# GpSimd issues the moves of the row maxima, SyncE keeps the moves of rows, and one key projection stands two steps sooner

## The reference

```
x = x + 0.5 * ffn(layernorm(x))            # 256 -> 2 x 768 -> 256, silu(gate) * up, int weights
x = x + attention(layernorm(x))            # 16 heads of 16, ALiBi bias -slope * |l - s|
x = x + 0.5 * ffn(layernorm(x))

attention(x): q, k, v = x Wq', x Wk', x Wv'
              scores = q k' / 4 + bias;  out = softmax(scores) v;  out Wo' + bo
```

## Time and profile before

| | |
|---|---|
| time, median of 3 runs | 805.88 us (804.81 to 812.14) |
| profiled execution | 807.18 us, of which the span from first to last instruction is 805.3 us |
| mean granted TensorE clock | 0.993 |
| busy: PE / DVE / ACT / POOL | 758.7 / 618.4 / 521.4 / 450.8 us |
| DMA queue of SP | 41.92 MB, 28.0% of 16 engines' span |

### The profile page before, as it was taken

How to read it: one execution, slowest core, us unless ns; L and a number is a source line. 1 busy time by engine, 2 the same in 40 slices (tenths; PEclk the granted TensorE clock), 3 DMA queues, 4 the chain that set the end, 5 groups by cost and what they waited for, 6 DMA issues and landing times.

```text
span 805.3 us, 13303 instructions
## 1 busy us (share of the span) xinstructions
PE 758.7 (94%) x4576; PEld 467.0 (58%) x4576; DVE 618.4 (77%) x1267; ACT 521.4 (65%) x1001; POOL 450.8 (56%) x550
## 2 busy tenths in 40 slices
PE   2999999999989999999999999999999997999998
PEld 1778887775443354444444454454443376988887
DVE  6698877967889968879878888879989076467763
ACT  5344444335868978878879879789788754344443
POOL 0433355425656767767766776767766555344433
PEclk9999999998999999999999999999999999999999
DMA  9440015401441650730721622522520000000001
GB/s 355 160 63 3 2 30 76 56 2 25 73 67 23 92 69 3 110 51 7 114 42 30 93 41 41 81 42 50 72 41 3 2 2 28 28 29 28 29 28 54
DMA packets 21637, 43.20 MB, mean 54 GB/s; under 512 B 3864, under 2 KB 5928, under 8 KB 21352
## 3 DMA queue, kind: packets, MB, share of 16 engines
q1 hardware_dynamic: 21544, 41.92, 28.0%
HBM read 12.02 MB, written 4.62 MB: 21 GB/s over the span
## 4 chain that ended last, share of the span: by engine, by line
PE 79%; ACT 7%; DVE 7%; issue 4%; DMA 1%; POOL 1%; DVEq 0%; ACTq 0%
PE ps L1003 73%; ACT probs L685 4%; PE ps L1066 2%; DVE row_max L881 2%; PE ps L1015 2%; DVE hid L811 1%; ACT stage L634 1%; PE ps L1071 1%; DMA q_aug<-parts 1%; DVE w_max L892 1%; ACT heads_t L669 1%; ACT xnt L652 1%; PE ps L1061 1%; DVE newton L732 1%; DMA x_sb<-x_in 0%
## 5 line engine op out<-in xcount | busy, mean ns | idle before, releaser
L881 DVE TENSOR_REDUCE row_max<-ps 128x1 f32<-128x512 f32 x512 | 326.6, 683 | 65.1 <-PE ps L1003 64.0
L685 ACT ACTIVATE probs<-ps 128x512 f32<-128x512 f32 x512 | 287.2, 607 | 49.3 <-PE ps L1003 47.6
L553 POOL TENSOR_TENSOR probs<-probs,diag 128x256 f32<-128x256 f32 x256 | 186.7, 731 | 131.7 <-ACT probs L685 130.9
L471 POOL TENSOR_TENSOR hid_r<-hid,hid_r 128x512 fp32r<-128x512 f32 x96 | 124.3, 1299 | 181.2 <-ACT hid_r L580 180.9
L1003 PE MATMUL ps<-k_aug,q_aug 60*128 60x512 f32 x512 | 191.3, 455 | 8.7 <-issue 3.8
L1003 PE MATMUL ps<-xnt,wgu_r 128*128 128x512 f32 x768 | 190.3, 402 | 7.9 <-issue 4.1
L1003 PE MATMUL ps<-q_aug,k_aug 62*128 62x512 f32 x512 | 191.6, 450 | 2.8 <-ACT probs L685 1.9
L1003 PEld LDWEIGHTS ps<-xnt,wgu_r 128*128 128x128 f32 x768 | 143.0, 190 | 46.3 <-issue 7.6
L1003 PEld LDWEIGHTS ps<-q_aug,k_aug 62*128 62x128 f32 x512 | 78.2, 186 | 120.6 <-ACT probs L685 97.6
L586 ACT ACTIVATE gated<-ps 128x512 f32<-128x512 f32 x96 | 57.4, 598 | 126.3 <-PE ps L1003 126.3
L1003 PE MATMUL ps<-probs,v_aug 128*32 128x512 f32 x1024 | 137.0, 608 | 0.1
(11 more groups left out here) (72 smaller groups left out, 672.3 us busy)
## 6 DMA issues: line engine op xcount, KB each, us to landing
q_aug<-parts SPq DMA_DIRECT2D x96, 128.0 KB, 4.6
k_aug<-parts SPq DMA_DIRECT2D x96, 128.0 KB, 4.6
x_sb<-x_in SPq DMA_DIRECT2D x8, 512.0 KB, 12.7
x_out<-x_sb SPq DMA_DIRECT2D x7, 512.0 KB, 2.6
diag<-diag_table SPq DMA_DIRECT2D x1, 2048.0 KB, 19.0
wgu_i<-w_gate_up SPq DMA_DIRECT2D x2, 768.0 KB, 6.0
w_att<-w_att SPq DMA_DIRECT2D x1, 1024.0 KB, 11.1
q_aug<-max_parts SPq DMA_DIRECT2D x64, 8.0 KB
```

Of the source, the lines that this page charges most:

```text
L471: nc.gpsimd.tensor_tensor(hid_r[:, 1, f, :], hid[:, f % 2, :], hid_r[:, 0, f, :].bitcast(F32), ALU.subtract).then_inc(s["hid_lo"], 1)
L553: nc.gpsimd.tensor_tensor(tile, tile, diag[:, kt % 2, n * QH + 2 * pair:n * QH + 2 * pair + 2, :], ALU.mult).then_inc(fixed, 1)
L685: nc.scalar.activation(probs[:, kt % 2, 2 * pair + i, :], score_bank(2 * g + i), ACT.Exp, scale=SLOPE_UNITS[pair]).then_inc(exp_done, 1)
L881: nc.vector.reduce_max(row_max[:, quad % 2, i, pair, t:t + 1], max_bank(b * MAX_TILES + tile), mybir.AxisListType.X).then_inc(s1_used, 1)
```

## The change

`move_max` leaves SyncE's program and is put, unchanged in what it moves, into GpSimd's, right behind `split_max`. SyncE's loop then holds only the row moves, in the order `qk0`, `qk1`, `qk2`, `qk3`. In the table of fills `qk1_next` and `turn0_prev` exchange their places: the key projection stands at (1, 1), the turn at (1, 3).

```diff
 FILLS = {
-    (1, 1): "turn0_prev", (1, 3): "qk1_next", (1, 4): "max2", (1, 5): "heads0", (1, 7): "qk2_next",
+    (1, 1): "qk1_next", (1, 3): "turn0_prev", (1, 4): "max2", (1, 5): "heads0", (1, 7): "qk2_next",
...
 (SyncE)
-            move_max(-1, "max0_next")
             sp.wait_ge(ffn[0]["y_used"], 2 * B)
             lay_k_rows(1)
             for b in range(B):
-                move_max(b, "max1")
                 if not last(b):
                     wait(sp, st_done, b * (2 * NQ * STEPS))
-                    move_rows(b, "qk0_next")
-                move_max(b, "max2")
-                if not last(b):
-                    move_rows(b, "qk1_next")
-                    move_rows(b, "qk2_next")
-                move_max(b, "max3")
-                if not last(b):
-                    move_rows(b, "qk3_next")
-                    move_max(b, "max0_next")
+                    for part in range(4):
+                        move_rows(b, f"qk{part}_next")
...
 (GpSimd)
+            def move_max(b, name):
+                seq, kind, part = fill_parts(b, name)
+                pool.wait_ge(max_split, seq * NQ + part + 1)
+                for o in range(2):
+                    at = ROW_MAX + o
+                    nc.gpsimd.dma_start(q_aug[seq % 2][at:at + GROUP + 1:GROUP, 2 * part:2 * part + 2, :].bitcast(F32).rearrange("i j (t p) -> i (j t) p", p=P),
+                                 max_parts[:, o, :].bitcast(F32)).then_inc(max_moved, 16)
...
             split_max(-1, "max0_next")
+            move_max(-1, "max0_next")
...
                         if s == 3 and FILLS[n, 4] in fills_of(b):
                             split_max(b, FILLS[n, 4])
+                            move_max(b, FILLS[n, 4])
```

More of the change, by code:

```diff
@@ L409, in move_rows @@
                                      ).then_inc(rows_moved[is_k], 16)
[L411 to L418, removed]
             lay_q_rows(0)
```

## The result

The changed kernel takes 848.35 us (median of 4 runs, 846.56 to 849.05) beside 807.18 us of the kernel before (4 runs, 804.81 to 812.14). The ratio is 1.0477 [1.0434, 1.0519]: 4.8% slower, where 0.4% had been forecast and a range of 798.9 to 828 us. The profiled execution took 846.56 us, with a span of 844.7 us.

The account below looks back on a forecast made before the run. TensorE was taken to set the pace; 10.7 us lost to late fixes against 7.1 us gained from its holes made 3.6 us slower, put on the 805.88 us median: 809.5 us, range 798.9 to 828 us.

Parts of the forecast that it names:

- the maxima's own deadline: At quad 2's first scores: maxima issued by GpSimd land at 333.0 us, 0.5 us in time.
- the maxima land late: Rival: maxima meet key rows, 0.2 us, hidden; or land 1 us later in every quad, 816 us; chance 0.05.
- late fixes: Fixes of steps 4 and 5 behind GpSimd's issues delay TensorE's weighing at the next quad's step 0; 10.7 us lost.
- Gain: TensorE's idle holes before tile 64 (quad 2, step 3) in blocks 0 to 5 vanish: 7.09 us won.
- The exchange costs nothing: Swapping the fills at (1, 1) and (1, 3) leaves TensorE the same matmuls within four steps; no cost found.
- The price of an issue on GpSimd: GpSimd's time for one DMA issue of the maxima, after `split_max`: estimated 1.04 us, between 0.549 and 1.288 us.
- T: GpSimd's delay per quad after `split_max`: two issues plus the wait for its own subtraction, 2.15 us.
- covers: Time between the end of step 5's fix and its weighing on TensorE, 1.05 to 2.27 us by quad.
- The cheap issue: Rival: a GpSimd issue costs SyncE's 0.549 us, T is 1.18 us, 7.0 us gain stay, 798.9 us; chance 0.22.
- The dear issue: Rival: a GpSimd issue costs 1.288 us, GpSimd bounds the turn of quads, 18.0 us slower, 823.9 us; chance 0.28.
- VectorE holding GpSimd: Rival: VectorE's layer-norm tiles at quad 1, step 4 delay GpSimd's issues, 4.9 us more, 814.4 us; chance 0.03.
- The key rows did come sooner: Denies the rival that GpSimd's work at (1, 1) or the queue holds the key rows, 813.6 us; chance 0.04.

Follow-up runs that it names:

- e2_sync_keys_first: Against the kernel before: the two fills exchanged, SyncE issues everything, all key DMAs ahead of `max2`; 836.0 us, ratio 1.0333.
- e4_split1: Against the kernel before: fills exchanged, SyncE issues everything, one key DMA ahead of `max2` and five behind; 800.68 us, ratio 0.9873; repeated 800.71 us, 0.9898.
- e1_no_swap: Against the changed kernel: the two fills put back, GpSimd still issues the maxima; 830.3 us, ratio 1.0255 to the kernel before.
- e9_pool_split1: Against the changed kernel: SyncE sends one key DMA, waits for the split of `max2`, sends five; 818.98 us, ratio 1.0131 to the kernel before.
- e5_half_keys: Against the changed kernel: only half the rows of each `qk1` DMA moved from block 1 on; 834.2 us, ratio 1.0355 to the kernel before.

## Why the prediction was wrong

**The step that failed** is the maxima's own deadline, and with it the rival "the maxima land late". The prediction let the moves land at most 1.1 us after their issue, taken from the kernel before, and priced their meeting with the key rows at one 128 KB DMA, 0.64 us, hidden. They met the rest of the query rows and all six key DMAs. In block 2 the issues end at 339.28 us and the maxima land 6.3 us later, not 1.1 us. The 0.64 us were the pace of issue; at the 126 to 129 GB/s of the windows 128 KB take 1.0 us. So the twelve row DMAs, issued in 7.6 us, need some 12.3 us to move (an estimate from these two numbers), and what is issued behind them finds what is left. TensorE's wait for the maxima, 25.0 us in all, is the first term; the mechanism had been given a chance of 0.05. The order on one queue alone makes it too (`e2_sync_keys_first`), and one key DMA instead of six takes it away (`e4_split1`).

The row that speaks against the forecast was in it: the earlier trace rows was read as saying that the query rows are over by 330 us and so cannot slow the keys. But the keys were to start at 327.4 us, and from 326 to 328 us the engines of the kernel before were still full of query rows, as its window there shows:

```profile
326.00:328.00 2.00, 2.00 (x14) 0.47 (x13) 1.08 (x3) 1.86 (x4) 1.03 (x2) 1.00 1.06 124
```

And the earlier trace rows says as much that the maxima had empty engines, and that the `max2` ahead of `qk1` on SP was not only a delay for the keys but what kept those engines empty. Moving the keys 3.6 us ahead put them there.

**The second term had no place in the sum**: a stalled TensorE. After waits of 3.2 to 4.2 us the clock is at its lower level for 3 to 10 us, and TensorE's busy time rises by 17.9 us. The prediction counted waits only.

**That it forecast "slower" at all** is luck: its 3.6 us came from late fixes against the holes. As measured, 3.6 us of late fixes, 2.7 us for `heads0` and 7.1 us gained make 0.8 us faster. The slowdown is the wait and the clock, which the sum did not hold.

**Gain**: right. None of the holes before tile 64 is left in blocks 0 to 5, and the key rows are issued right behind the query rows. The changed kernel alone does not prove it, since TensorE comes to tile 64 later there, behind its wait for the maxima; `e4_split1`, without that wait, shows that the gain is to be had.

**The exchange costs nothing**: not quite. `heads0` now comes before ScalarE has taken `max_row`, 0.44 us in six of the blocks, 2.7 us in all by the waits; alone, the exchange measures 1.0016 [0.9986, 1.0046].

**The price of an issue on GpSimd**: mis-sized upwards, 1.04 us forecast, 0.584 us measured in the median; T is 0.30 + 1.16 = 1.46 us, not 2.15 us. The 1.0 us that the prediction also tried is not a hold of GpSimd: with free engines the first packet moves 1.2 us after the issue begins (`e1_no_swap`), and as late after an issue on SyncE in the kernel before. By the prediction's covers a T of 1.46 us loses 0.05 us before the weighing of quad 0 of the next block, nothing in quad 1 and 0.41 + 0.12 us in block 7. Measured are 0.16 to 0.35 us at the first place in five blocks and 1.13 us at the turn from block 6 to block 7, none in quad 1 of blocks 0 to 6, and in block 7 nothing at its first place and 0.89 us at its second: 3.6 us in all, against 7 x 0.05 + 0.53 = 0.9 us by the covers at this T. The covers were 0.1 to 0.3 us shorter than read at the turn of a block, 1.1 us at the turn to block 7, and 0.8 us at block 7's second place; at its first place the cover was longer than read.

**The other rivals.** The cheap issue came true by its own condition, but its 798.9 us needed the maxima in time. The dear issue, and VectorE holding GpSimd, are out: of 64 issues the longest took 0.898 us, and with free engines the moves landed 2.6 us after their issue at most (`e1_no_swap`). The key rows did come sooner. The Trainium skill (SBUF — State Buffer, section SBUF: two separate sides) has VectorE keep GpSimd from writing its descriptors under some operations; nothing in this kernel shows it.

**What stays open.** How the 39 us split between wait and clock was read from the records, not set by an experiment: `e2_sync_keys_first` has nearly the same waits (23.2 us), but 763.7 us of busy time and a clock of 0.981. There the clock is at its lower level for 3.4 to 6.8 us after six of the seven waits, in the changed kernel for up to 10.2 us after all seven; why it recovers sooner, no run says. And that the moves on GpSimd's queue were held until the rows ahead of them had drained is observed; what orders them inside the DMA engines is not seen. `e9_pool_split1` fits both an order of arrival and queues that take turns.

## What to carry to other kernels

A small, urgent DMA is priced by the bytes issued ahead of it on the same engines, on whichever queue: before taking a wait out of a queue, look whether that wait keeps the engines free for what follows it. Here 128 KB ahead was free (`e4_split1`), and 768 KB cost 3% (`e2_sync_keys_first`). Where two engines would have to agree on that order, let one issue both, as in `e4_split1`, and count for a TensorE that stalls for some us the slower clock behind the stall as well.

## What the runs showed of the hardware

- GpSimd issues a small DMA about as fast as SyncE: 0.584 us against 0.549 us in the median, though its elementwise work is 1.9 times as slow as VectorE's.
- In the changed kernel a second queue was no way past rows issued ahead. The DMA view of the changed kernel in three single us of block 2 (queue: packets, MB, share), 340 to 341, 342 to 343 and 343 to 344 us:

```profile
q1 hardware_dynamic: 78, 0.13, 109.2%
...
q1 hardware_dynamic: 78, 0.13, 108.4%
...
q0 software_dynamic: 56, 0.02, 20.6%
```

  GpSimd's moves, issued from 338.12 to 339.28 us, have no packet on the engines before 343 us, when the rows of SyncE's queue run out. In blocks 0 to 6 the first packet of `max2` came 3.7 to 5.1 us after its issue began, with free engines 1.2 us. The Trainium skill (DMA: Bandwidth & Descriptors, section Queues, rings and completion order) has each DMA engine take turns, packet by packet, between the queues that have work. By that rule the maxima would have passed between the rows and most of the 25.0 us of waiting would not be there; the measurement decides against it for rows issued ahead. In `e9_pool_split1`, where the rows were issued level with the maxima, the first packet came after 1.5 us and the small packets did go between the rows.
- Halving the rows of a DMA about halved its pace too: the DMA share fell from 1.1 to 0.58 (`e5_half_keys`).
- After each of the seven waits of 3.2 to 4.2 us in the changed kernel TensorE's granted clock was 0.50 for 3 to 10 us.
- VectorE's multiplication of `heads` (128x256), 0.99 us at most in the kernel before, took up to 4.30 us in the changed kernel and 5.68 us in `e1_no_swap`, both times beside a GpSimd that worked without a gap. What held it no run says.
